# A recommender tower in fp32 on one core: GpSimd drains its gathers ahead of the waits for transposed rows, and waits for two groups at a time

## The reference

```python
e = stack([tbl_f[ids[:, f]] for f in 27 features])          # 2048 x 27 x 128, fp32
interactions = einsum('bfd,bgd->bfg', e, e)                 # per sample, 27 x 27
x = interactions[:, lower triangle without the diagonal]    # 351 pairs
h = concatenate([bottom, x, bottom], axis=1)                # 128 + 351 + 128 = 607
h = relu(h @ W_top1 + b_top1)                               # 512
h = relu(h @ W_top2 + b_top2)                               # 256
y = h @ W_top3                                              # 2048 x 1
```

## Time and profile before

| | |
|---|---|
| median of 3 runs | 410.1 us (408.98 to 410.92) |
| the profiled execution | 408.56 us, span 406.8 us |
| PE busy | 357.0 us, 88% |
| POOL busy | 250.9 us, 62% |
| DVE busy | 220.1 us, 54% |
| granted TensorE clock, mean | 0.966 |
| gathers, L417 | 240, 1042 ns each in the mean |

### The profile page before, as it was taken

How to read it: one execution, slowest core, us unless ns; L and a number is a source line. 1 busy time by engine, 2 the same in 40 slices (tenths; PEclk the granted TensorE clock), 3 DMA queues, 4 the chain that set the end, 5 groups by cost and what they waited for, 6 DMA issues and landing times.

```text
span 406.8 us, 9934 instructions
## 1 busy us (share of the span) xinstructions
PE 357.0 (88%) x3895; PEld 301.1 (74%) x3895; DVE 220.1 (54%) x524; ACT 158.7 (39%) x257; POOL 250.9 (62%) x247
## 2 busy tenths in 40 slices
PE   0770776789699999999999999999999999977997
PEld 0550654678588879889788889799688798876795
DVE  0760687784369984524298983233689835300400
ACT  2321243565224354453334354453243643621533
POOL 5777287677777777777775777777727776000000
PEclk9985799999989999999999999999999999988999
DMA  6999233482655552336454633355445523211100
GB/s 188 232 249 259 72 88 82 134 205 66 160 138 137 127 120 69 86 94 160 138 122 106 138 93 72 83 148 153 112 99 121 127 62 80 53 51 30 24 2 0
DMA packets 60681, 45.55 MB, mean 112 GB/s; under 512 B 31711, under 2 KB 51687, under 8 KB 60635
## 3 DMA queue, kind: packets, MB, share of 16 engines
q1 hardware_dynamic: 51332, 27.39, 28.2%
q0 software_dynamic: 7680, 15.74, 15.8%
q10 hardware_dynamic: 1623, 1.79, 1.8%
HBM read 40.03 MB, written 4.85 MB: 110 GB/s over the span
## 4 chain that ended last, share of the span: by engine, by line
PE 75%; DMA 6%; SPq 6%; DVE 6%; ACT 4%; issue 2%; ACTq 0%
PE ps_build L735 38%; PE ps_dense L782 10%; PE ps_gram L759 9%; PE ps_dense L811 7%; DMA id_raw<-ids_onehot_dram 4%; SPq L296 3%; PE ps_gram L744 3%; ACT embT L569 2%; DVE table L434 2%; PE ps_dense L819 2%; DMA gram_dram<-gram 2%; PE ps_build L744 2%; DVE hot L457 1%; ACT table L558 1%; SPq L297 1%
## 5 line engine op out<-in xcount | busy, mean ns | idle before, releaser
L417 POOL DMA_INDIRECT rows<-tbl_dram,idx x240 | 250.1, 1042 | 92.1 <-issue 69.2
L735 PE MATMUL ps_build<-hot,table 125*128 125x512 f32 x768 | 191.2, 404 | 35.7 <-DVE hot L457 35.1
L735 PEld LDWEIGHTS ps_build<-hot,table 125*128 125x128 f32 x768 | 144.1, 193 | 73.4 <-issue 29.0
L457 DVE TENSOR_SCALAR hot<-id_raw 125x512 fp32r<-125x512 f32 x384 | 154.0, 443 | 55.3 <-PE ps_build L735 51.1
L569 ACT COPY embT<-ps_build 128x512 f32<-128x512 f32 x48 | 57.9, 1207 | 141.3 <-PE ps_build L735 136.2
L759 PE MATMUL ps_gram<-embT 128*53 128x52 f32 x1792 | 48.5, 217 | 4.7 <-DVE gram L465 3.9
L759 PEld LDWEIGHTS ps_gram<-embT 128*53 128x53 f32 x1792 | 46.8, 132 | 7.0 <-issue 5.4
L465 DVE COPY gram<-ps_gram 117x416 f32<-117x416 f32 x28 | 15.5, 587 | 37.6 <-DMA gram_dram<-gram 23.0
L782 PE MATMUL ps_dense<-pairT,w1p 120*128 120x256 f32 (+1 forms) x252 | 35.6, 288 | 0.0
L448 DVE TENSOR_SCALAR id_raw<-id_raw,vocab 125x512 f32<-125x512 int32 x48 | 23.4, 488 | 18.3 <-DMA id_raw<-ids_onehot_dram 18.3
L782 PEld LDWEIGHTS ps_dense<-pairT,w1p 120*128 120x128 f32 (+1 forms) x252 | 33.1, 197 | 0.0
(11 more groups left out here) (61 smaller groups left out, 131.4 us busy)
## 6 DMA issues: line engine op xcount, KB each, us to landing
id_raw<-ids_onehot_dram SPq DMA_DIRECT2D x144, 64.0 KB
raw<-tbl_dram SPq DMA_DIRECT2D x12, 448.0 KB
gram_dram<-gram SPq DMA_DIRECT2D x56, 84.5 KB
rows<-tbl_dram,idx POOLq DMA_INDIRECT x240
id_raw<-ids_onehot_dram SPq DMA_DIRECT2D x12, 256.0 KB
bot<-bottom_dram SPq DMA_DIRECT2D x7, 128.0 KB, 2.4
w1p_raw<-w_pairs_dram ACTq DMA_DIRECT2D x1, 720.0 KB
raw<-tbl_dram SPq DMA_DIRECT2D x12, 52.0 KB
```

The lines of the kernel that those rows point to most:

```text
L417: nc.gpsimd.indirect_dma_start(rows[:, t % 2, s * D:(s + 1) * D], None, tables[f], bass.IndirectOffsetOnAxis(idx[:, TILES * i + t, f:f + 1 ...
L457: nc.vector.tensor_scalar(hot[0:VP, a % HOT_SLOTS, :], shifted, float(v), None, ALU.is_equal).then_inc(hot_made, 1)
L735: last = nc.tensor.matmul(bank[:, :], table[0:VP, n, bits, v * D:(v + 1) * D], hot[0:VP, a % HOT_SLOTS, :], start=(v == bits == 0), stop=( ...
```

## The change

Two things are changed in `gather`. The wait for transposed rows is made ahead of groups 0 and 2 only, and asks for the later of two groups (0 and 1, or 2 and 3). Ahead of each such wait stands a drain of GpSimd: its sequencer goes on only when the engine has finished what is queued. There are two waits and two drains in each of the tiles 2 to 15, 28 drains in all.

```diff
                 for u in range(TQ):
                     h, before = (i, t - 2) if t >= 2 else (i - 1, t + 2)
-                    if h >= 0:
-                        pool.wait_ge(built, BUILDS * h + nth("rows", before, u) + 1)
+                    if h >= 0 and u % 2 == 0:
+                        nc.gpsimd.drain()
+                        pool.wait_ge(built, BUILDS * h + nth("rows", before, u + 1) + 1)
                     pool.sem_inc(gathers_begun, 1)
```

## The result

The changed kernel takes **460.75 us** in the median of 4 runs (456.83 to 463.63), the kernel before 409.94 us (408.98 to 410.92). The ratio is 1.123, with a 95% interval of 1.114 to 1.132: 51 us slower. The forecast was 486, in a range of 460 to 508: the sign and the mechanism were right, the size was too large by half, and the number lies at the very edge of the range.

A forecast was written before the change was run, and what follows sets the result against it. PE bounds the kernel, POOL close behind; 27 drains at 3.7 us (99.9), less 11.5 slack, plus 0.4, delay the last transposes 79 us; corrections -4 and +2 make 77 on 408.56: 485.6, said as 486 us, range 460 to 508.

The forecast's parts named there:

- What bounds the kernel: PE sets the block's period; POOL (GpSimd) is second bound, 5 us per block behind, with 11.5 us of slack.
- The pair wait: Wait for group 1 where group 0 was asked: costs 0.4 us, once, against the first transposes.
- The drain waits for the data: GpSimd's drain is held until the last gather's data land and a bit, 2.78 us past the gather's end.
- the rival of the cheap drain: Mid-stream drains cost only a 0.6 us restart each; SP's later reads delay PE: 410 to 416 us, chance 0.06.
- The other two rivals on the drain: First: shorter landing, 1 to 2 us, giving 432 to 460, chance 0.05. Second: landing over 4 us, above 515, chance 0.03.
- The price of a drain: POOL's loss per drain: 2.78 held, 0.9 restart, less 0.30, plus 0.3 for the crowd: 3.7 us.
- The 0.3 us for the crowd of SP's transfers: Added per drain for slower landing while SP's queue loads the DMA engines more; an estimate without a row.
- The sum: POOL's last gather ends at 343.8 + 99.9 - 11.5 + 0.4 = 432.6; last transposes begin 79 us later.
- The correction of 4 us for gathers that meet less of DVE: Gathers' excess time blamed on DVE; its work spread over a sixth more time saves 4 us.
- Where the time stands: PE's idle time goes to waits for gathers ahead of L744, 80 us in all, most at tile 3.
- The coupling through SP: In block 1, SP's ids for one-hot unit 7 wait for tile 6's gathers; POOL longer by 5 us, so hidden.
- The clock: PE pauses lower the granted clock; only the part just behind the last gather shows, 2 us more.

The follow-up runs named there:

- the memset: Changed kernel with a tiny GpSimd memset and a wait for its semaphore in place of each drain: 411.9 us, ratio 1.009 to the kernel before.
- the kernel without pacing: Changed kernel in which SP no longer waits for handed-over gathers before its reads of pairs and ids: 463.9 us, ratio 1.136 to the kernel before.
- 56 drains: Changed kernel with a drain ahead of every group from the third tile on, pair waits kept: 530.1 us, kernel before 571.0, disturbed session.
- the kernel with 14 drains: Changed kernel with drains ahead of group 0 alone, one a tile: 431.2 us, ratio 1.058 to the kernel before; disturbed sessions 584.6, 585.5 and 568.4 us.
- the kernels with 56 and 28 drains: The 28: changed kernel's drains, but the four waits a tile of the kernel before: 543.6 us, kernel before 571.0, disturbed session.

## Why the prediction was right, and where its size was off

**The number.** 460.75 lies 0.75 us above the lower end of the range, and under the 465 at which the forecast's own range began; one of the four runs took 456.83. That it still falls inside is luck: the price of a drain, 2.84 us, is below the 3.0 to 4.5 from which the range was worked out, and its lower end of 3.0 gives 467 by the forecast's own sum.

**What bounds the kernel.** Right: GpSimd was the second bound with 11.5 us of slack, and 27 gaps were enough to make it the first. After the first drain it never waits for PE again.

**The pair wait** at 0.4 us: right. PE comes to the second group 0.44 us after the first (49.49 and 49.93), a part of the 1.8 us by which the first gap is longer; the rest is PE's own later start. In the time of the kernel with the pair wait alone it can't be seen.

**The drain waits for the data.** Right, and the rival of the cheap drain fell; the memset shows what it would have been, 411.9, inside the 410 to 416 given. The Trainium skill's "VectorE: DVE Perf Modes", on the DRAIN you can't avoid, gives its 12 ns for boilerplate drains alone, those at a program's start and end. No such drain on GpSimd is that short behind gathers, neither the 17.85 us of the earlier trace rows nor that of the changed kernel:

```profile
L125 POOLq DRAIN  x1: 7506/7506/7506, 401.8 to 401.8; - x1
```

Of a drain that a program itself asks for on GpSimd it states nothing there; the 28 took 7.1 us at least, the gathers still queued included.

**The other two rivals on the drain.** The landing was neither shorter nor over 4 us: 1.97 in the mean and 3.42 at most, where the last one of the kernel before took 1.68. Still the first of the two came nearer with its price, 1.6 to 2.6 us, than the forecast with 3.7: the drain ended 2.31 us behind the gather, for another reason than the rival's.

**The price of a drain was the step that failed.** 3.7 us were put down, and 3.14 - 0.30 = 2.84 measured. 27 times the difference is 23 us, and the forecast has 22 too much: 485.6 was worked out for the profiled execution and 463.6 came. The term that was mis-sized is the drain's own rest between the landing and its end. The drain of 2.78 us at the program's end was not a fair sample: it consists of 1.68 us to the last landing and 1.11 behind that, and the 1.11 is 0.34 in the changed kernel. The 0.3 us for the crowd of SP's transfers, which no row had shown, came out in size, 1.97 in place of 1.68, though no run shows that the crowd is the reason. The restart was put at 0.9 and took 0.82.

**The sum.** Its form holds. With the measured gaps: 343.8, plus 65.0 (the 27 gaps, 84.7 us, less the 19.6 that stood there before, waits included), plus 1.8 for the longer first gap and 0.2 for a later start, less 3.8 for shorter gathers, is 407.0 against 406.9. The correction of 4 us for gathers that meet less of DVE came out as 3.8, and the traces agree with its reason: a gather during which DVE executes nothing takes 0.95 us in the mean in both kernels (67 of the 240 before, 74 after), the others 1.08 and 1.06. The stretch behind the last gather, given 2 + 51.2 + 2 = 55.2, took 54.9.

**Where the time stands.** Wrong. PE was to wait 80 us ahead of L744; it waits 1.6 us for rows there, and 61.8 at the one-hot units, where 35.1 stood before. The coupling through SP was to be hidden by 5 us in block 1: GpSimd 51.9 from tile 6's first gathers to tile 7's last, PE 47. In the trace the two sides meet. GpSimd hands over tile 6 from 155.94 on and ends tile 7 at 204.04, 48.1 us; its last group lands at 207.46, and PE transposes it at once:

```profile
207.60 0.52 PE L745 MATMUL ps_build<-ident,rows 128*128 128x128 f32 x3
```

0.14 us behind a landing is also where PE begins its transposes in the kernel without pacing when it waits for rows, so here the rows still ended last. In blocks 2 and 3 PE comes 1.2 and 2.5 us behind the landing of the same group, so there it was not the rows. Nothing of the 5 us was left. The cheaper drain took nearly 3 of them (3 x 0.86); what took the others was not separated. The run without pacing shows that it made no difference to the time.

**The clock.** The 2 us for it can't be told apart from the rest. It fell as expected: 0.926 in the mean of the span, 0.966 before, and PE is busy for 16.2 us longer with the same 3895 matmuls, 14.6 of it at the one-hot units (205.8 us at L736, 191.2 at L735 before).

## What to carry to other kernels

In these runs a drain of GpSimd behind gathers costs the landing of the last one and a restart, some 2.8 us over the usual step, also when nothing depends on it; if the queue only has to be empty, a small instruction and its semaphore do it for 0.8. Before an engine is called idle at 60%, add up what passes between its instructions: here 0.30 us per gather make 62% of the span into 94% of the time up to the last gather ((250.1 + 239 x 0.30) / 340.5). And price a wait by its smallest parts (landing, rest, restart), not by one sample at the program's end.

## What the runs showed that was not expected

**The drain's rest grows with what it drains.** From the last landing to the drain's end it took 0.16 to 0.21 us with three or four gathers since the last drain (56 drains), 0.32 to 0.37 with seven or eight (28), and 0.65 with fifteen (14), about 0.04 us for each gather. In the profile it is the smallest gaps that show it: 2.47, 2.66 and 3.01 us. Behind the first drain of the changed kernel, after 30 gathers, it is 1.11, and at the end of the kernel before, after 240 with no drain between, it is 1.11 too: it does not grow on without end. That is why the one drain that the first trace had was too dear a model.

**A session in which PE is held up while GpSimd gathers.** On the same chip, minutes after a session with 404 to 413 us, the kernel before took 563 to 580. The trace of the kernel with 14 drains in such a session shows it best; the waits of PE and a piece of its timeline:

```profile
PE ps_build L737 <- issue: 46.8, 36, 4.3
PE ps_gram L761 <- issue: 45.8, 76, 1.7
```

```profile
263.03 0.32 PE L761 MATMUL ps_gram<-embT 128*53 128x52 f32 x3 [0.49 <-issue]
263.77 0.35 PE L761 MATMUL ps_gram<-embT 128*53 128x52 f32 x2 [0.43 <-issue]
264.51 0.47 PE L761 MATMUL ps_gram<-embT 128*53 128x52 f32 x5 [0.38 <-issue]
```

PE gets two to five matmuls every 0.7 us and waits for no semaphore in between. From 115 us to the last gather it was idle for 37% of the time in which gathers ran, the 0.30 us between two counted in, and for 10% of the rest. There the kernels with 56 and 28 drains were faster than the one without: 530 and 544 us against 565 to 571; with 14 it was 568 to 586. What disturbed these sessions is open; no run was made that could tell.
